# A routing sort's later products in fp32r, its weights as a high and a low part

## The reference, cut to what matters

```
rw = softmax(router_logits);  w, sel = top_k(rw, 2);  w = w / w.sum(-1)
dense_w[b, sel[b]] = w[b]
out = sum over e of dense_w[:, e] * mlp(x, skill_gate[e], skill_up[e], skill_down[e])
out = out + mlp(x, shared_gate, shared_up, shared_down)
mlp(x, g, u, d) = (gelu(x @ g) * (x @ u)) @ d
x = x + out          (x is here already the result of the first layer)
```

## Time and profile before

| | us |
|---|---|
| median of 3 runs | 130.94 |
| lowest, highest | 130.9, 131.74 |
| the profiled execution | 130.7 |
| its span | 129.0 |
| TensorE busy in the span | 124.4 |
| VectorE, ScalarE, GpSimd busy | 90.4, 72.3, 61.4 |

### The profile page before, as it was taken

One profiled execution on the slowest core, in us unless ns is written; L12 is line 12 of the kernel. 1 busy time (PEld: TensorE's weight loads), 2 busy tenths in 40 slices (PEclk: granted clock), 3 DMA queues, 4 the chain that ended last, 5 costly groups with the idle time before them and its releaser, 6 DMA issues.

```text
span 129.0 us, 3154 instructions
## 1 busy us (share of the span) xinstructions
PE 124.4 (96%) x869; PEld 113.3 (88%) x869; DVE 90.4 (70%) x177; ACT 72.3 (56%) x136; POOL 61.4 (48%) x111
## 2 busy tenths in 40 slices
PE   6999999999999999999999999999999999999991
PEld 6657887878887889999999999999999999999990
DVE  2767988769979999543478767767777677766641
ACT  2484667976956777113566476557665756611110
POOL 5649464553796977552253643553365413610000
PEclk9999999999999999999999999999999999999999
DMA  3998888899000057589555586558799950023921
GB/s 55 271 332 298 292 239 275 231 295 283 21 3 0 0 194 286 175 323 422 239 224 231 196 333 262 208 201 307 264 323 315 381 180 0 3 73 97 287 64 53
DMA packets 14524, 26.56 MB, mean 206 GB/s; under 512 B 2224, under 2 KB 7600, under 8 KB 12976
## 3 DMA queue, kind: packets, MB, share of 16 engines
q1 hardware_dynamic: 14192, 26.35, 59.8%
q10 hardware_dynamic: 320, 0.07, 0.3%
HBM read 12.52 MB, written 1.31 MB: 107 GB/s over the span
## 4 chain that ended last, share of the span: by engine, by line
PE 91%; DVE 3%; DMA 1%; issue 1%; POOL 1%; DVEq 0%; POOLq 0%
PE bank L1044 11%; PE bank L1080 9%; PE bank L1081 9%; PE bank L1082 9%; PE bank L1062 6%; PE bank L991 6%; PE bank L993 6%; PE bank L992 6%; PE bank L1102 5%; PE bank L1103 4%; PE bank L1104 4%; PE bank L1007 3%; PE bank L1008 3%; PE bank L1009 3%; PE bank L916 3%; PE bank L924 2%
## 5 line engine op out<-in xcount | busy, mean ns | idle before, releaser
L556 ACT ACTIVATE work<-bank 128x512 f32<-128x512 f32 x48 | 28.7, 598 | 39.2 <-PE bank L1082 17.5
L714 DVE TENSOR_TENSOR bank<-bank,work 128x512 f32<-128x512 f32 x40 | 27.9, 699 | 18.3 <-PE bank L1082 13.1
L731 DVE TENSOR_TENSOR hT_lo<-bank,hT_hi 128x512 fp32r<-128x512 f32 x40 | 27.3, 682 | 1.0 <-issue 0.5
L1080 PE MATMUL bank<-xp,wst 128*128 128x256 f32 x96 | 27.3, 284 | 0.0
L1081 PE MATMUL bank<-xp,wst 128*128 128x256 f32 x96 | 27.2, 283 | 0.0
L1082 PE MATMUL bank<-xp,wst 128*128 128x256 f32 x96 | 27.2, 283 | 0.0
L483 POOL TENSOR_TENSOR wstd<-wexd,wstd 128x512 fp32r<-128x512 f32 x12 | 15.5, 1294 | 24.3 <-ACT wstd L598 24.3
L565 ACT CAST hT_hi<-bank 128x512 fp32r<-128x512 f32 x40 | 23.3, 583 | 1.6 <-DVE bank L714 1.6
L1081 PEld LDWEIGHTS bank<-xp,wst 128*128 128x128 f32 x96 | 18.4, 192 | 0.0
L1080 PEld LDWEIGHTS bank<-xp,wst 128*128 128x128 f32 x96 | 18.4, 192 | 0.0
L1082 PEld LDWEIGHTS bank<-xp,wst 128*128 128x128 f32 x96 | 18.4, 192 | 0.0
(11 more groups left out here) (153 smaller groups left out, 211.9 us busy)
## 6 DMA issues: line engine op xcount, KB each, us to landing
wst<-wex SPq DMA_DIRECT2D x12, 1024.0 KB, 4.7
raw_ex<-n_L_cond_skill_gate_dram SPq DMA_DIRECT2D x8, 256.0 KB, 3.1
raw_ex<-in_L_cond_skill_up_dram SPq DMA_DIRECT2D x8, 256.0 KB, 3.8
sst<-n_L_cond_skill_gate_dram SPq DMA_DIRECT2D x8, 256.0 KB, 3.7
sst<-in_L_cond_skill_up_dram SPq DMA_DIRECT2D x8, 256.0 KB, 4.2
xn<-in_x_dram SPq DMA_DIRECT2D x4, 256.0 KB, 4.3
out_dram<-xT SPq DMA_DIRECT2D x4, 256.0 KB, 2.7
sst<-_L_cond_shared_gate_dram SPq DMA_DIRECT2D x1, 256.0 KB, 4.6
```

Of the source, the lines that this page charges most:

```text
L556: act.activation(gelu_sb[q], gate_ps[q][:, :], ACT.Gelu_apprx_tanh).then_inc(gelu_done, 1)
L714: dve.tensor_tensor(up_ps[u][:, :], up_ps[u][:, :], gelu_sb[q], ALU.mult).then_inc(h_done, 1)
L731: dve.tensor_tensor(hT_lo[:, q, :], up_ps[u][:, :], f32(hT_hi[:, q, :]), ALU.subtract).then_inc(lo_done, 1)
L1080: pe.matmul(of_c, w_hi, x_hi, start=True, stop=False)
```

## The change

The three later groups of the sort's products (`sort_starts`, `sort_singles`, `sort_lists`) read fp32r tiles. For this, copies are added: three constants on GpSimd early on, `half` on VectorE, `twice` on GpSimd; `par` is written as fp32r at once. The row of weights is made twice: `w_parts` holds the weight in fp32r and what is left of it, each gets its rows, so there are two more small operations and eight row operations instead of six, and the lists' products are four: two of 96 columns and two of 32 that add the low part onto the weights. The counts that others wait for move along (`S_CLASS` 16 to 17, `S_ROWS` 32 to 37). The `zeros` tile of the warm-up moves into a part of `wstd`, and `n_ge` shares its place with `rows`.

```diff
--- before.py
+++ after.py
@@ -62,7 +62,6 @@
         bias = sb("bias", [H, 1])
         ident = sb("ident", [P, P])
         ones = sb("ones", [B, P])
-        zeros = sb("zeros", [P, P])
         bT = sb("bT", [P, H])
         wT = sb("wT", [H, H])
         cond_er = sb("cond_er", [B, E, R])
@@ -77,21 +76,29 @@
         bcol = sb("bcol", [B, 1])
         ltri = sb("ltri", [B, B])
         upick = sb("upick", [B, 3, 8])
+        ltri_r = sb("ltri_r", [B, B], F32R)
+        upick_r = sb("upick_r", [B, 3, 8], F32R)
+        ones_r = sb("ones_r", [B, P], F32R)
         memb = sb("memb", [B, 2, B])
         memb_sum = sb("memb_sum", [B, B])
         rank_n = sb("rank_n", [B, 2, B])
-        n_ge = sb("n_ge", [B, B, 8])
         half = sb("half", [B, B])
-        par = sb("par", [B, B])
+        half_r = sb("half_r", [B, B], F32R)
+        par_r = sb("par", [B, B], F32R)
         starts = sb("starts", [B, 3, 8])
         pos_e = sb("pos_e", [B, 4, 8])
         pos_ke = sb("pos_ke", [B, 2, 8])
         pos = sb("pos", [B, 2])
         single = sb("single", [B, 2])
         twice = sb("twice", [B, 4])
+        twice_r = sb("twice_r", [B, 2], F32R)
         left_rank = sb("left_rank", [B, 4])
         lp = sb("lp", [B, 16])
-        rows = sb("rows", [B, 2, 3, 32])
+
+        with nc.sbuf_tensor("n_ge", [B, B, 8], F32) as n_ge:
+            pass
+        rows = sb("rows", [B, 2, 4, 32], F32R)
+        w_parts = sb("w_parts", [B, 2, 2], F32R)
         wlist = sb("wlist", [P, 32])
         idx = sb("idx", [1, 64], I32)
 
@@ -119,6 +126,7 @@
         hT_lo = sb("hT_lo", [P, 2, I], F32R)
         xs = sb("xs", [P, NBUF, S])
         wstd = sb("wstd", [P, NBUF, 2, DN], F32R)
+        zeros = wstd[:, NBUF - 1, 1, 0:P].bitcast(F32)
 
         with nc.sbuf_tensor("raw_ex", [P, E, 2, I], F32) as raw_ex:
             pass
@@ -246,7 +254,7 @@
         P_PAD, P_TWO_B, P_SLOT_EB, P_TWO_E, P_FOUR_E, P_FOUR_B, P_SIX_PART, P_SIX_B = range(1, 9)
 
 
-        S_MEMB, S_PAR, S_POS, S_CLASS, S_ROWS = 3, 5, 11, 16, 32
+        S_MEMB, S_PAR, S_POS, S_CLASS, S_ROWS = 3, 5, 11, 17, 37
 
         block = ctx.enter_context(nc.Block())
 
@@ -363,6 +371,11 @@
             pool.wait_ge(sort_step, 2)
             pool.tensor_tensor(memb_sum[:, :], memb[:, 0, :], memb[:, 1, :], ALU.add).then_inc(sort_step, 1)
 
+
+            pool.tensor_copy(ltri_r[:, :], ltri[:, :]).then_inc(consts, 1)
+            pool.tensor_copy(ones_r[:, :], ones[:, :]).then_inc(consts, 1)
+            pool.tensor_copy(upick_r[:, :, :], upick[:, :, :]).then_inc(consts, 1)
+
             pool.wait_ge(setup_sb, 2)
             for g in range(2, NG):
                 pool.tensor_tensor(sB[:, g, :, :],
@@ -395,9 +408,9 @@
             pool.memset(base[:, :, :], 0.0).then_inc(base_zero, 1)
 
             pool.wait_ge(sort_sum, 2)
-            pool.tensor_scalar(par[:, :], half[:, :], -2.0, None, ALU.mult).then_inc(sort_step, 1)
+            pool.tensor_scalar(par_r[:, :], half[:, :], -2.0, None, ALU.mult).then_inc(sort_step, 1)
             pool.wait_ge(sort_step, 4)
-            pool.tensor_tensor(par[:, :], par[:, :], rank_n[:, 1, :], ALU.add).then_inc(sort_step, 1)
+            pool.tensor_tensor(par_r[:, :], f32(par_r[:, :]), rank_n[:, 1, :], ALU.add).then_inc(sort_step, 1)
 
 
             pool.wait_ge(sort_sb, 2)
@@ -417,7 +430,7 @@
 
 
 
-            pool.wait_ge(sort_sum, 3)
+            pool.wait_ge(sort_sum, 4)
             pool.tensor_scalar(single[:, :], pos[:, :], float(LEFT), None, ALU.is_ge).then_inc(sort_step, 1)
             pool.wait_ge(sort_step, 12)
             pool.tensor_tensor(twice[:, 0:1], single[:, 0:1], single[:, 1:2], ALU.mult).then_inc(sort_step, 1)
@@ -426,6 +439,8 @@
             pool.tensor_scalar(twice[:, 3:4], twice[:, 0:1], -2.0, None, ALU.mult).then_inc(sort_step, 1)
             pool.wait_ge(sort_step, 15)
             pool.tensor_tensor(twice[:, 1:2], twice[:, 2:3], twice[:, 3:4], ALU.add).then_inc(sort_step, 1)
+            pool.wait_ge(sort_step, 16)
+            pool.tensor_copy(twice_r[:, :], twice[:, 0:2]).then_inc(sort_step, 1)
             x1_whole(1)
             up_lo(0, 1)
             up_lo(1, 2)
@@ -434,25 +449,30 @@
             pool.wait_ge(sort_sb, 3)
             pool.tensor_tensor(lp[:, 0:1], left_rank[:, 1:2], left_rank[:, 2:3], ALU.add).then_inc(sort_step, 1)
             pool.tensor_tensor(lp[:, 1:2], left_rank[:, 0:1], left_rank[:, 2:3], ALU.subtract).then_inc(sort_step, 1)
-            pool.wait_ge(sort_step, 18)
+            pool.wait_ge(sort_step, 19)
             pool.tensor_tensor(lp[:, 2:3], left_rank[:, 0:1], lp[:, 0:1], ALU.subtract).then_inc(sort_step, 1)
             pool.tensor_scalar(lp[:, 4:5], lp[:, 1:2], lp[:, 0:1], 8.0, ALU.subtract, ALU.add).then_inc(sort_step, 1)
             pool.tensor_scalar(lp[:, 5:6], lp[:, 0:1], float(LEFT), None, ALU.add).then_inc(sort_step, 1)
-            pool.wait_ge(sort_step, 21)
+            pool.wait_ge(sort_step, 22)
             pool.tensor_copy(lp[:, 3:4], lp[:, 4:5]).then_inc(sort_step, 1)
-            pool.wait_ge(sort_step, 22)
+            pool.wait_ge(sort_step, 23)
             pool.tensor_scalar(lp[:, 6:8], lp[:, 2:4], twice[:, 0:1], lp[:, 5:6], ALU.mult, ALU.add).then_inc(sort_step, 1)
-            pool.wait_ge(sort_step, 23)
+            pool.wait_ge(sort_step, 24)
             pool.tensor_tensor(lp[:, 8:10], lp[:, 6:8], pos[:, :], ALU.subtract).then_inc(sort_step, 1)
-            pool.wait_ge(sort_step, 24)
+            pool.wait_ge(sort_step, 25)
             pool.tensor_tensor(lp[:, 10:12], lp[:, 8:10], single[:, :], ALU.mult).then_inc(sort_step, 1)
-            pool.wait_ge(sort_step, 25)
+            pool.wait_ge(sort_step, 26)
             pool.tensor_tensor(lp[:, 12:14], lp[:, 10:12], pos[:, :], ALU.add).then_inc(sort_step, 1)
-            pool.wait_ge(sort_step, 26)
+            pool.wait_ge(sort_step, 27)
 
             pool.wait_ge(rt_step, RT_WEIGHTS)
+            pool.tensor_copy(w_parts[:, 0, :], rt[:, 22:24]).then_inc(sort_step, 1)
+            pool.wait_ge(sort_step, 28)
+            pool.tensor_tensor(w_parts[:, 1, :], rt[:, 22:24], f32(w_parts[:, 0, :]), ALU.subtract).then_inc(sort_step, 1)
+            pool.wait_ge(sort_step, 29)
             for k in range(2):
-                for i, value in enumerate((top_idxf[:, k:k + 1], bcol[:, 0:1], rt[:, 22 + k:23 + k])):
+                for i, value in enumerate((top_idxf[:, k:k + 1], bcol[:, 0:1], f32(w_parts[:, 0, k:k + 1]),
+                                           f32(w_parts[:, 1, k:k + 1]))):
                     pool.tensor_scalar(rows[:, k, i, :], iota[:, :], lp[:, 12 + k:13 + k], value,
                                        ALU.is_equal, ALU.mult).then_inc(sort_step, 1)
             x1_whole(2)
@@ -769,6 +789,8 @@
                                           ALU.is_ge).then_inc(sort_sum, 1)
                         dve.wait_ge(sort_sum, 1)
                         dve.tensor_reduce(half[:, :], n_ge[:, :, :], AXIS_X, ALU.add).then_inc(sort_sum, 1)
+                        dve.wait_ge(sort_sum, 2)
+                        dve.tensor_copy(half_r[:, :], half[:, :]).then_inc(sort_sum, 1)
                     if g == 0 and c == 2:
                         gate_lo(0)
                     if g == 0 and c == 3:
@@ -933,23 +955,26 @@
                 pe.matmul(count_ps[0:B, B:2 * B], memb_sum[:, :], ones[:, 0:B], start=True, stop=True).then_inc(sort_mm, 1)
 
             def sort_starts():
-                pe.wait_ge(sort_sum, 2)
+                pe.wait_ge(sort_sum, 3)
+                pe.wait_ge(consts, 11)
                 pe.wait_ge(sort_step, S_PAR)
                 pe.wait_ge(x1lo_ready, NG)
-                pe.matmul(start_ps[0:B, 0:24], half[:, :], upick[:, :, :].rearrange("p a e -> p (a e)"),
+                pe.matmul(start_ps[0:B, 0:24], half_r[:, :], upick_r[:, :, :].rearrange("p a e -> p (a e)"),
                           start=True, stop=False)
-                pe.matmul(start_ps[0:B, 8:16], par[:, :], ltri[:, 0:8], start=False, stop=True).then_inc(sort_mm, 1)
+                pe.matmul(start_ps[0:B, 8:16], par_r[:, :], ltri_r[:, 0:8], start=False, stop=True).then_inc(sort_mm, 1)
 
             def sort_singles():
                 pe.wait_ge(sort_step, S_CLASS)
-                pe.matmul(rank_ps[0:B, 0:2], ltri[:, :], twice[:, 0:2], start=True, stop=True)
-                pe.matmul(rank_ps[0:B, 2:4], ones[:, 0:B], twice[:, 0:2], start=True, stop=True).then_inc(sort_mm, 1)
+                pe.matmul(rank_ps[0:B, 0:2], ltri_r[:, :], twice_r[:, 0:2], start=True, stop=True)
+                pe.matmul(rank_ps[0:B, 2:4], ones_r[:, 0:B], twice_r[:, 0:2], start=True, stop=True).then_inc(sort_mm, 1)
 
             def sort_lists():
                 pe.wait_ge(sort_step, S_ROWS)
                 for k in range(2):
-                    mm = pe.matmul(list_ps[:, 0:96], ones[:, :], rows[:, k, :, :].rearrange("b v n -> b (v n)"),
-                                   start=(k == 0), stop=(k == 1))
```

(4 more changed lines are left out.)

## The result

The changed kernel takes 133.47 us (median of 4 runs, 132.56 to 134.12), the kernel before 130.92 on the same occasion: ratio of all runs 1.0172, 95% interval 1.0123 to 1.0221 (the two medians alone give 1.0195). The forecast was 131.5 with a range of 130.3 to 132.5, and a chance of 0.77 that the change stays within 1%. The kernel is slower by more than was allowed for.

What follows compares the result with a forecast made beforehand. TensorE, busy 96%, was taken as the bound. About 0.3 us saved at starts and singles, a 1.4 us list wait and list products of 0.71 instead of 0.95 gave +0.77 on 130.7: 131.5 us, range 130.3 to 132.5.

Steps and rivals of the forecast that it cites:

- What bounds the kernel: Whole kernel: TensorE, busy 96% of the span; a microsecond it must wait is added to the end.
- Early edits at nothing: Before the sort products: added constant copies, moved tiles and copies of half and twice cost 0, hidden by idle time.
- Starts and singles: TensorE at these two places: fp32r products save 0.14 + 0.13, about 0.3 us in all; bounds 0 to 0.75.
- The price of a record: TensorE's sort products: 0.12 us for each fp32r product, taken from products of 256 columns.
- The lists' chain: GpSimd before the list products: rows end at 39.99, first list product at 40.04, a new TensorE wait of 1.4 us.
- GpSimd's frame: Start of GpSimd's work for the lists: moves earlier by 0 to 1.24 us, taken as 0.3.
- The late release of VectorE after the fp32 singles: VectorE's gated product at 28.99 started 0.49 us after the product it waited for; might go with fp32r.
- The collision with VectorE's gate split: GpSimd's rows for the lists: one row operation stands still beside VectorE's L736; 0.5 us taken, bounds 0 to 0.68.
- The list products: TensorE at the lists: four one-record products, 0.71 us from the first to L1008 instead of 0.95; bounds 0.3 to 0.95.
- The sum: Lists to end: +0.77 us at L1008, no further TensorE wait; GpSimd's lateness of 1.5 to 2 us harmless; 131.5.
- Rival 2: At the lists: fp32r products no cheaper, wait paid in full, collision 0.68; +1.49 us, 132.2; chance 0.14.
- Rival 3: After the lists: the 1.4 us wait drops TensorE's clock to 1.2 GHz, 4 us of it giving 133.5; chance 0.04.

Runs made afterwards that it cites:

- the probe: Changed kernel plus four more 16 by 16 by 24 products at starts in fp32r and four at singles in fp32; one run, stretch 115.99 us.

## Why the prediction was wrong

**What bounds the kernel:** right. Both waits of TensorE were added to the end in full: 0.59 and 1.85 us in the stretch, with nothing given back.

**Early edits at nothing:** right for the constants (L368's idle time fell from 0.84 to 0.33 us) and for the copy of twice.

**Starts and singles:** mis-sized. Forecast savings 0.14 and 0.13, measured 0.84 - 0.78 and 0.83 - 0.78, 0.06 and 0.05. The price of a record was taken from products of 256 columns; a product this small costs 0.028 us, and the place 0.26.

**The lists' chain:** right in kind and near in size. The rows end at 38.43 + 1.28 = 39.71, forecast 39.99. GpSimd's frame moved more than I took: its split stands at 30.64 instead of 31.02 in a trace that began 0.16 us later, so 0.54 against my 0.3. The late release of VectorE after the fp32 singles went away: L734 starts at 28.61, 0.05 after the end of L1018 (28.17 + 0.39), not 0.49. Four fp32 products put at singles ahead of the fp32r ones did not bring it back (0.05 again), so its cause is open. The collision with VectorE's gate split was there and cost 0.37 (two rows operations in 1.28 us where two take 0.91), forecast 0.5. The list products cost 40.64 - 39.76 = 0.88 us to L1033, forecast 0.71, before 0.95. That the low product came out within 0.27 us of the forecast is luck in part: GpSimd's frame and the collision were both better than forecast, the list products worse.

**The sum:** this step failed. It said that after L1008 TensorE has no further wait, that the other engines follow it, and that GpSimd, late by 1.5 to 2 us, is needed next only for the singles' inputs: a cost of 0. Measured was 1.85 us, the larger part of the 2.44. GpSimd's lateness was followed to who waits for it, and not to whom it stands in the way of. VectorE's pack waits for nothing of GpSimd's; before, it asked 0.07 us ahead of the end of a GpSimd operation, now it asks 0.25 us into one. Held for 2.1 us, it holds VectorE's queue: the split, the gated product and the sum of the group, for which TensorE stands. The lateness was mis-sized as well. Counted from the first shared product, GpSimd's sum behind the rows started 1.24 us late (39.68, before 38.28), but the sum beside the pack only 0.24 (43.90, before 43.50) and the singles' inputs 0.20 (46.38, before 46.02), because it no longer stood idle 0.7 us ahead of each of two splits. The prediction had the evidence, a VectorE split of 1.78 us beside a GpSimd sum, and used it in one direction and for one place.

**Rivals:** none of them was what happened. Rival 2, the one for slower by more than 1%, asked for list products without any gain and a collision of 0.68, and neither was so. Rival 3's clock stayed full here, so that its 133.5 is the measured median is chance; with a wait of 3.09 us the clock did fall. The Trainium skill ("SBUF — State Buffer", "SBUF: two separate sides") says that a VectorE operation with two SBUF inputs and a GpSimd operation that reads SBUF block each other for the whole instruction. Six traces agree, with packs of 0.36 to 3.73 us. By the rows the lock isn't sharp at its edge: before, the pack (43.47 to 43.64) ran beside a GpSimd sum listed from 43.50.

**Open:** which end of a GpSimd operation lets VectorE in. It was the first in two traces (0.95 and 0.36 us), the second in three (2.30, 2.31 and, in the probe, 2.27), and a later one in the one with GpSimd late (3.73). In all of them GpSimd's next operation is listed close behind. One thing goes with it in the rows: in the two traces with one end, as in the three of before, GpSimd had stood idle 0.7 us for VectorE ahead of the last split before the pack; in the four others it came from the lists' rows without a pause. That this is the cause isn't shown.

## What to carry to other kernels

When an edit moves one engine in time, late or early, follow the shift to the end of the stage, and ask at each of its operations not only who waits for it but which short operation of another engine now stands beside it and can be held up, as the pack was here. A tiny operation in front of a long queue is the one to protect: give it an operand from PSUM, or let the other engine wait for it. And if a chain of tiny operations feeds the engine that bounds the kernel, count the operations before adding any; four row operations in place of eight took 1.5 us in place of 4.0 here.

## What the runs showed of the hardware

- A VectorE operation with two SBUF operands, 0.17 us long alone, took 0.36 to 3.73 us beside back-to-back GpSimd operations, and up to three of those ended without letting it in. With one operand from PSUM it took 0.16 us beside a running GpSimd operation.
- TensorE's clock stayed at its upper level after a standstill of 1.81 us, and after a standstill of 3.25 us it fell within the first product to the lower level, 1.2 GHz (granted 0.50), for 3.4 us: nine products of 512 columns, most of them 0.43 us apart instead of 0.23.
- A product of 16 by 16 by 24 in the stream costs 0.028 us in fp32r and 0.075 in fp32. Putting a pair of such products between two of 128 rows costs 0.22 to 0.26 us on top; what part of it waits, weight loads and sizes have isn't shown.
